# Attention and a gated feed-forward: x loaded turned and normalised so by GpSimd, projections dealt out anew, reciprocals of the row sums spread through DRAM

## What is computed

```python
x = x + tanh(g_xattn) * attention(layernorm(x), ctx, mask)     # 8 batches, 512 rows, D = 512, 16 heads of 32
x = x + tanh(g_ffn) * ffn(layernorm(x))
# attention: Q = layernorm(x) Wq' + bq, K = ctx Wk' + bk, V = ctx Wv' + bv, softmax with a mask, P V, output projection
# ffn:       r = sigmoid(mix_r Wr'), k = relu(mix_k Wk')^2, out = r * (k Wv'); mix = mu*x + (1-mu)*(x of the row before)
```

## Time and profile before

| | |
|---|---|
| median of three executions | 1231.34 us (1231.12 to 1231.93) |
| profiled execution | 1232.68 us, its span 1230.8 us |
| TensorE, VectorE, ScalarE, GpSimd busy | 1167.7, 942.5, 745.2, 237.4 us (95, 77, 61, 19%) |
| TensorE's granted clock, mean | 0.99 of full |
| DMA | 110.33 MB, 31% of the 16 engines' time |

### The profile page before, as it was taken

The page is one execution under the profiler, slowest core; times in us unless marked ns, Lnnn a source line. Parts: engine busy times, 40 slices in busy tenths (PEclk is TensorE's granted clock), DMA queues, the critical chain, the costliest instruction groups (busy, mean ns, idle before and its releaser), DMA issues.

```text
span 1230.8 us, 22178 instructions
## 1 busy us (share of the span) xinstructions
PE 1167.7 (95%) x7424; PEld 921.5 (75%) x7424; DVE 942.5 (77%) x2011; ACT 745.2 (61%) x1619; POOL 237.4 (19%) x427
## 2 busy tenths in 40 slices
PE   3999999999999999999999999977999999999997
PEld 2777776777777777777677777754888888888886
DVE  5778788788878887878878887879677677777763
ACT  4578778678768877877867876764432333233232
POOL 2030030030021003003003000024423433332431
PEclk9999999999999999999999999987999999999999
DMA  6433342253243333344225322452111311311200
GB/s 218 120 94 83 101 122 66 63 157 81 71 129 89 81 102 100 82 104 118 67 60 159 78 74 65 123 168 76 59 52 60 95 52 52 104 52 52 97 25 35
DMA packets 72703, 110.33 MB, mean 90 GB/s; under 512 B 14864, under 2 KB 23696, under 8 KB 72592
## 3 DMA queue, kind: packets, MB, share of 16 engines
q1 hardware_dynamic: 72592, 108.92, 31.1%
HBM read 41.76 MB, written 16.78 MB: 48 GB/s over the span
## 4 chain that ended last, share of the span: by engine, by line
PE 76%; DVE 9%; issue 6%; ACT 4%; DMA 4%; SPq 1%; POOL 0%; POOLq 0%; ACTq 0%; DVEq 0%
PE bank L445 24%; PE bank L509 14%; PE bank L476 12%; PE bank L521 10%; PE bank L502 7%; PE bank L485 6%; DMA x_rows<-x 3%; DVE neg_s L857 3%; ACT probs L681 2%; PE bank L491 2%; PE bank L575 1%; DVE pT L863 1%; DVE xh L973 1%; DMA pT<-wkT 1%; DVE ctx_sb L848 1%
## 5 line engine op out<-in xcount | busy, mean ns | idle before, releaser
L681 ACT ACTIVATE probs<-neg_s,negmax 128x512 f32<-128x512 f32 x512 | 367.9, 720 | 40.5 <-DVE negmax L857 39.4
L857 DVE CUSTOM_DVE_ANT_0 neg_s<-bank,mask_big 128x512 f32<-128x512 f32 x512 | 344.7, 683 | 19.2 <-PE bank L502 16.9
L509 PE MATMUL bank<-ident,probs 128*128 128x128 f32 x2048 | 314.8, 276 | 17.3 <-ACT probs L681 16.8
L509 PEld LDWEIGHTS bank<-ident,probs 128*128 128x128 f32 x2048 | 240.4, 141 | 75.6 <-ACT probs L681 40.7
L863 DVE COPY pT<-bank 128x512 f32<-128x512 f32 x256 | 176.5, 690 | 120.8 <-PE bank L509 119.7
L502 PE MATMUL bank<-k_stack,q_stack 96*128 96x512 f32 x512 | 243.3, 475 | 6.0 <-DVE negmax L857 5.9
L688 ACT COPY pT<-bank 128x512 f32<-128x512 f32 x256 | 149.4, 584 | 98.3 <-PE bank L509 92.5
L1068 POOL TENSOR_SCALAR var_eps<-mv 128x2 f32<-128x2 f32 (+1 forms) x24 | 18.5, 770 | 639.9 <-DVE mv L822 578.3
L521 PE MATMUL bank<-pT,v_sb 128*32 128x512 f32 x1024 | 118.5, 603 | 0.8 <-issue 0.5
L779 ACT ACTIVATE relu<-bank 128x512 f32<-128x512 f32 x32 | 19.2, 598 | 149.0 <-PE bank L445 149.0
L502 PEld LDWEIGHTS bank<-k_stack,q_stack 96*128 96x128 f32 x512 | 97.3, 190 | 11.2 <-DVE negmax L857 8.5
(11 more groups left out here) (110 smaller groups left out, 2125.1 us busy)
## 6 DMA issues: line engine op xcount, KB each, us to landing
k_stack<-k_hi SPq DMA_DIRECT2D x256, 64.0 KB, 2.0
q_stack<-q_hi SPq DMA_DIRECT2D x256, 64.0 KB, 2.0
x_rows<-x SPq DMA_DIRECT2D x8, 1024.0 KB, 6.6
cT_raw<-ctxT SPq DMA_DIRECT2D x8, 1024.0 KB, 5.8
k_stack<-k_lo SPq DMA_DIRECT2D x128, 64.0 KB, 2.0
q_stack<-q_lo SPq DMA_DIRECT2D x128, 64.0 KB, 2.0
ctx_dram<-ctx_sb SPq DMA_DIRECT2D x32, 256.0 KB, 2.1
c_raw<-ctx_dram SPq DMA_DIRECT2D x16, 512.0 KB, 5.1
```

The source lines that it names most:

```text
L509: mm = nc.tensor.transpose(pt_bank[i % 2][:, a * P:(a + 1) * P], probs[:, i % P_RING, a * P:(a + 1) * P], ident[:])
L681: nc.scalar.activation(probs[:, i % P_RING, :], neg_s[:, i % SM_RING, :], ACT.Exp, bias=negmax[:, k:k + 1], scale=-1.0, accum_out=den[:, g ...
L857: nc.vector.tensor_tensor_reduce(neg_s[:, i % SM_RING, :], s_bank[i % S_BANKS][:], mask_big[:, q, :], 1.0, 3e38, ALU.add, ALU.min, negmax[ ...
```

## The change

x is also passed turned (`xT_d`). From the second batch on, SyncE loads rows of x only for the statistics, one row of four to a partition, two tiles at a time, then x turned, also two at a time into the other half of the same buffer; mean and inverse root go to DRAM and come back spread over all partitions. GpSimd subtracts, scales and takes the rests of x and of the context; ScalarE rounds both at steps given by `x_hi_at` and `c_hi_at`. The T and C items are left in the prologue alone. K, Q and V are dealt out as one of each per group; Q 3 moves to steps 6 to 9 of group 1, so that x may be overwritten. The statistics of batch nb are taken at steps 8 and 10 of group 3 of batch nb-2 and steps 3 and 5 of group 0 of batch nb-1. The reciprocals are turned as they are (16 columns, one transpose), copied by VectorE at step 2 (into `ctx_sb`), stored to DRAM and loaded with 32 partitions for each head, four loads, which stand in SyncE's queue behind the first copies of Q; the product follows at step 7, and the context's store behind all of the stacking. At the end of the first stage the last product waits for its own trip. Semaphore counts, the order of the three side banks, and loops that were written as b in range(B-1) and a last one follow suit.

```diff
@@ -55,14 +55,11 @@
 
 
 PE_SIDE = [
-    parts("K", 1, 0, 1, 3, 4) | parts("V", 2, 6, 7, 8, 9, 10, 11) | parts("Q", 2, 12, 13, 14, 16),
-    parts("K", 2, 0, 1, 3, 4) | parts("V", 3, 6, 7, 8, 9, 10, 11) | parts("Q", 3, 12, 13, 14, 16),
-    {step: [("T", n, 0, 1)] for n, step in enumerate((0, 1, 3, 4))} | parts("K", 3, 5, 6, 7)
-    | parts("Q", 4, 9, 10, 12, 13, 14, 16),
-    parts("K", 4, 0, 1, 2) | parts("V", 0, 3, 4, 5, 6) | parts("V", 1, 7, 8, 9, 10)
-    | parts("Q", 5, 11, 12, 13, 14, 15, 16),
+    parts("K", 1, 0, 1, 3, 4) | parts("V", 1, 5, 6, 7, 8, 9, 10) | parts("Q", 2, 12, 13, 14, 16),
+    parts("K", 2, 0, 1, 3, 4) | parts("Q", 3, 6, 7, 8, 9) | parts("V", 2, 10, 11, 12, 13, 14, 15),
+    parts("K", 3, 0, 1, 3, 4) | parts("V", 3, 5, 6, 7, 8, 9, 10) | parts("Q", 4, 12, 13, 14, 16),
+    parts("K", 4, 0, 1, 3, 4) | parts("V", 0, 6, 7, 8, 9, 10, 11) | parts("Q", 5, 12, 13, 14, 16),
 ]
-PE_SIDE[2][TILES] += [("C", n, 0, 1) for n in range(CH)]
...
-STATS_STEPS = (8, 10, 12, 14)
-HI_STEP, LO_STEP = 1, 2
+def stats_at(nb):
+    return ((0, 0, 8), (0, 0, 10), (0, 1, 1), (0, 1, 3)) if nb == 1 else (
+        (nb - 2, 3, 8), (nb - 2, 3, 10), (nb - 1, 0, 3), (nb - 1, 0, 5))
+def x_hi_at(nb):
+    return ((0, 2, 0), (0, 2, 1), (0, 2, 7), (0, 2, 8)) if nb == 1 else (
+        (nb - 1, 1, 10), (nb - 1, 1, 11), (nb - 1, 2, 2), (nb - 1, 2, 3))
+def c_hi_at(nb):
+    return tuple((nb - 1, 2, i) for i in (11, 12, 13, 14))
+HI_STEP, LO_STEP, DIVIDE_STEP = 1, 2, 7
 HI_SIDE, LO_SIDE = out_side(0, HI_STEP), out_side(1, LO_STEP)
-EARLY = LO_STEP + 1
 C_ITEMS, T_ITEMS = [("C", n) for n in range(CH)], [("T", n) for n in range(TT)]
-PROLOGUE = C_ITEMS + [("K", 0)] + T_ITEMS + [("Q", 0), ("V", 0), ("V", 1), ("Q", 1)]
-NEXT_BATCH = C_ITEMS + T_ITEMS + [("Q", 4), ("K", 4), ("V", 0), ("V", 1), ("Q", 5)]
+PROLOGUE = C_ITEMS + [("K", 0)] + T_ITEMS + [("Q", 0), ("V", 0), ("Q", 1)]
+NEXT_BATCH = [("Q", 4), ("K", 4), ("V", 0), ("Q", 5)]
...
+        rden_rows = [ctx_sb[0:TILES, s, 0:P] for s in range(2)]
...
+            def load_rows(b, t):
+                if b == 1:
+                    sp.wait_ge(side_done, done(side_no(None, ("T", TT - 1))))
+                else:
+                    sp.wait_ge(x_lo, (b - 1) * CH)
+                if t >= 2:
+                    sp.wait_ge(bn_done, b * TT + t - 1)
+                sp.dma_start(x_rows[:, t % 2, :],
+                             x[bass.ds(b * S, S), :].rearrange("(p t) c -> t p c", t=TT)[t]).then_inc(rows_ld[t % 2], 16)
+            def load_xT(b, a):
+                if b > 1 or a >= 2:
+                    sp.wait_ge(x_lo, (b - 1) * CH + (a - 1 if a >= 2 else 0))
+                sp.dma_start(x_rows[:, 2 + a % 2, :], xT_d[bass.ds(b * D + a * P, P), :]).then_inc(xT_ld[a % 2], 16)
+            def broadcast_mean_rstd(b):
+                sp.wait_ge(mr_copy, b)
+                sp.wait_ge(pool_chain, (b + 1) * CHAIN)
+                sp.dma_start(mr_dram[b].rearrange("(k p t) -> p k t", k=2, p=P), mean_rstd[:]).then_inc(mr_st, 16)
+                sp.wait_ge(mr_st, b * 16)
+                sp.dma_start(x_rows[:, 0:2, :].rearrange("p k t -> p (k t)"),
+                             mr_dram[b:b + 1, :].to_broadcast([P, 2 * S])).then_inc(mr_ld, 16)
...
                 first = GH if n == GROUPS - 1 else GH - 1
                 stack_q(b, n, range(first))
+                if b * GROUPS + n > 1:
+                    load_rden(b * GROUPS + n - 2)
                 stack_k(b, n, (0,))
...
+            def store_rden(b, c):
+                sp.wait_ge(side_done, done(side_no(b, ("R", c))))
+                sp.dma_start(rden_dram[b * GROUPS + c].rearrange("(r q) -> r q", r=TILES),
+                             rden_rows[c % 2]).then_inc(rden_st, 16)
+            def load_rden(g):
+                sp.wait_ge(rden_st, (g + 1) * 16)
+                sp.wait_ge(ctx_done, g)
+                for j in range(GH):
+                    sp.dma_start(rden_bc[j * HD:(j + 1) * HD, :],
+                                 rden_dram[g:g + 1, j * S:(j + 1) * S].to_broadcast([HD, S])).then_inc(rden_ld, 16)
             def store_context(b, c):
-                sp.wait_ge(side_done, done(side_no(b, ("R", c))))
+                sp.wait_ge(ctx_done, b * GROUPS + c + 1)
                 sp.dma_start(ctx_dram[bass.ds(b * D + c * P, P), :], ctx_sb[:, c % 2, :]).then_inc(ctx_st[c % 2], 16)
             def batch(b):
                 for c in range(GROUPS):
-                    if c == 0 and not is_last(b):
-                        sp.wait_ge(side_done, done(b * SIDE_PER_BATCH + len(PROLOGUE) - 1))
-                        load_x(b + 1)
-                    if c:
-                        store_context(b, c - 1)
+                    if b + c == 0:
+                        load_rows(1, 0)
+                        load_rows(1, 1)
+                        load_xT(1, 0)
+                        load_xT(1, 1)
+                    if b + c:
+                        store_rden(*((b, c - 1) if c else (b - 1, GROUPS - 1)))
                     if not (is_last(b) and c == GROUPS - 1):
                         sp.wait_ge(s_mm, tile_no(b, c, 0) + HEAD)
...
                             sp.wait_ge(side_mm, mm_no(b, ("Q", c + 1)) + 1)
                             load_w2(0)
                         stack_group(b, c + 1)
+                    else:
+                        load_rden(b * GROUPS + c - 1)
+                    if b + c:
+                        store_context(*((b, c - 1) if c else (b - 1, GROUPS - 1)))
                     if c == 0 and not is_last(b):
                         load_ctx(b + 1)
+                    if b == 0 and c == 0:
+                        load_rows(1, 2)
+                        load_rows(1, 3)
+                    if c == (1 if b == 0 else 0) and not is_last(b):
+                        broadcast_mean_rstd(b + 1)
+                    if c == 1 and not is_last(b):
+                        load_xT(b + 1, 2)
+                        load_xT(b + 1, 3)
+                    if c == GROUPS - 1 and b + 2 < B:
+                        for t in range(TT):
+                            load_rows(b + 2, t)
+                        load_xT(b + 2, 0)
+                        load_xT(b + 2, 1)
...
+                if part == 0 and (kind, n) == ("Q", 4):
+                    pe.wait_ge(x_lo, (b + 1) * CH)
+                if part == 0 and (kind, n) == ("K", 4):
+                    pe.wait_ge(ct_lo, (b + 1) * CH)
...
-                    for q in range(TT):
-                        mm = nc.tensor.transpose(bank[:, q * P:(q + 1) * P],
-                                                 rden_rep[:, q].rearrange("p j d -> p (j d)"), ident[:])
+                    mm = nc.tensor.transpose(bank[0:TILES, 0:P], rden[:], ident[:])
...
-                pe.wait_ge(side_done, previous_r(b, c))
+                pe.wait_ge(ctx_done, b * GROUPS + c)
...
+            def x_rounded(nb, a):
+                act.wait_ge(side_mm, mm_no(nb - 1, ("Q", GROUPS - 1)) + 1)
+                act.wait_ge(x_hat, (nb - 1) * CH + a + 1)
+                nc.scalar.copy(act_hi[0][:, a, :], x_rows[:, 2 + a % 2, :]).then_inc(x_hi, 1)
+
+            def c_rounded(nb, a):
+                act.wait_ge(side_mm, mm_no(nb - 1, ("V", 3)) + 1)
+                act.wait_ge(c_ld, nb * 16 + 16)
+                nc.scalar.copy(act_hi[1][:, a, :], cT_raw[:, a, :]).then_inc(ct_hi, 1)
...
-                if t == 0:
-                    dve.wait_ge(x_ld, b * 16 + 16)
-                    dve.wait_ge(mv_done, b * TT)
-                nc.vector.bn_stats(stats[:, t, :], x_rows[:, t, :]).then_inc(bn_done, 1)
+                if b:
+                    dve.wait_ge(rows_ld[t % 2], ((b - 1) * 2 + t // 2 + 1) * 16)
+                else:
+                    dve.wait_ge(x_ld, 16)
+                dve.wait_ge(mv_done, b * TT)
+                nc.vector.bn_stats(stats[:, t, :], x_rows[:, t % 2 if b else t, :]).then_inc(bn_done, 1)
...
+                if kind == "R":
+                    dve.wait_ge(side_mm, mm_no(b, item) + 1)
+                    dve.wait_ge(ctx_st[n % 2], (b * 2 + n // 2) * 16 + DMA_HEAD)
+                    nc.vector.tensor_copy(rden_rows[n % 2], bank[0:TILES, 0:P]).then_inc(side_done, 1)
...
+            def divide(b, c):
+                g = b * GROUPS + c
+                dve.wait_ge(rden_ld, (g + 1) * GH * 16)
+                dve.wait_ge(pv_mm, g + 1)
+                nc.vector.tensor_tensor(ctx_sb[:, c % 2, :], pv_bank[:], rden_bc[:], ALU.mult).then_inc(ctx_done, 1)
...
-                dve.wait_ge(rden_ready, g + HEAD)
-                nc.vector.reciprocal(rden[:], den[:, c % 2, :]).then_inc(rden_calc, 1)
-                dve.wait_ge(rden_calc, g + 1)
-                src = rden[:].rearrange("p (j q) -> p q j", j=GH)[:, :, :, None].to_broadcast([P, TT, GH, HD])
-                nc.vector.tensor_copy(rden_rep[:], src).then_inc(rden_ready, 1)
+                nc.vector.reciprocal(rden[:], den[:, c % 2, :]).then_inc(rden_ready, 1)
...
```

(54 more changed lines are left out.)

149 lines of the change are left out of this document (62 added, 87 removed).

## The result

The changed kernel takes **1447.09 us** (median of four runs, 1446.53 to 1457.27) against 1231.63 for the kernel before beside it (1231.12 to 1232.03). The ratio is 1.177, with a 95% interval of 1.172 to 1.182. The forecast said 1367 with a range up to 1407. The direction was right; the size, +215 us where +136 was forecast, lies outside the range.

What follows compares the result with a forecast made beforehand. TensorE was taken to bound attention, thinly. Gain -51, product 17.5 + 38 + 2.8, Q3 40, statistics 67, clock 15, once-only 5 + 2: +136 us on the median of 1231.34, so 1367, range 1292 to 1407.

Steps and rivals of the forecast that it cites:

- the clock: TensorE at 1.2 GHz after the idle in group 3: 2.5 us for each of six, 15; bounds 0 and 6.8.
- S+6.1: SyncE's queue in group (3,1): the nine q copies end 6.1 us after S, the release of the reciprocals' store.
- S+10.2: SyncE's queue in group (3,1): the spread reciprocals are there 10.2 us after S, the release of their store.
- -51: The change's gain together: 48 us over seven batches, prologue -2.8, last batch's third group +0.3.
- the ends: Prologue loses a V item (-2.8); last reciprocals' trip delays VectorE (+4), early c_raw gives back about 2 (+2).
- (2): Attention: T gone and V items dealt anew, 4 x 23.25 = 93.0 against 99.9 a batch, 48 us over seven.
- up to 1.6 a batch if its cover is gone: ScalarE's roundings, four of 0.6, only move beside tiles 11 to 14: 0, up to 1.6 a batch uncovered.
- TensorE has about a tile in hand: Product at step 7: work in hand also covers the product (0.68), so wait minus 0.3 charged; group 0 2.5.
- the landing of the rows: Statistics at step 8 of group 3: row loads take 2.1 to land; VectorE stands 11.7 us, 67 charged for six batches.
- B: Only Q3's and the statistics' waits decide; the product's is hidden, the clock stays: 1294 us, chance 0.17.
- C: Neighbours' reserve absorbs the waits; late work is caught up before the PV block: 1211 us, chance 0.06.
- D: Low clock through the tiles after each stall (+26), x late in groups 1 and 2 (+14): 1407 us, chance 0.15.

Runs made afterwards that it cites:

- E7: The kernel before, with only the reciprocals' DRAM trip (one transpose per group) and the product at step 12: 1220.42 us, ratio 0.991.
- E3: E2 with all four heads' q copies ahead of k's for Q2 too: 1252.38 us, ratio 1.016.
- E5: E3 with the trip of mean and inverse root ahead of the 1 MB context load in batches 1 to 6: 1238.44 us, ratio 1.005.
- E9: E8 with the first batch's trip of mean and inverse root behind K's first head in SyncE's group 1: 1229.3 us, ratio 0.999.
- E8: E5 with V2 at steps 5 to 8 and Q3 at 9 to 12 of group 1, x's roundings moved too: 1235.76 us, ratio 1.003.
- E6: E5 with the reciprocals as in the kernel before (four transposes, product at step 2), leaving x's new way and dealing: 1230.87 us, ratio 0.998.
- E4: The changed kernel with idle identity transposes on TensorE at step 10, and more at step 11 of fourth groups, to keep its clock up: 1429.48 us, ratio 1.160.
- E2: E1 with the product with the spread reciprocals at step 12 instead of 7: 1282.28 us, ratio 1.041.
- E1: The changed kernel with the loads of batch b+2's first two row tiles ahead of the stacking copies in SyncE's group 3: 1392.13 us, ratio 1.130.
- E10: E7 with the product put back from step 12 to step 7: 1361.03 us, ratio 1.103.

## Why the prediction was right in direction and short in size

**What held.** All of the waits were where the prediction put them. The product waited 4.0 us on average in group 0, 3.2 in group 3 and 4.6 in group 2, where 3.1, 3 and 5 were said; the statistics stood 10.6 us behind a first wait of 2.7 in (3,3), where 8 to 9 behind 3 were said; ScalarE stood for the queries in all eight groups 1; the fourth group took 39.8 us where "34 us or more" was said, TensorE's share fell to 84% where some 85% was said, and the clock's digits fell below 9. One sign came in number but not in size: ScalarE's waits were to be 2 to 5 us, and seven of the eight were 0.5 to 1.2. The places on SyncE's queue, S+6.1 for the q copies and S+10.2 for the reciprocals, were right within half a microsecond. That part came from one sum: copies of 0.62 us, counted in the order in which the code issues them. The direction and nearly nine tenths of the waits' size (165 of 188.7 us) came from it. The gain of one transpose for four, 0.3 us a group, was right too (E7, 0.33).

**The thirty groups, as they came out.** 745.7 us became 952.4. No run has the change's own dealing without any wait, so its base is put together here: groups 0, 2 and 3 as in E3 (24.0, 24.8 and 23.8 us), group 1 at the 24.6 us of E5 without its wait (23.9 in batch 7, from E3), and (0,2) from E9. These come to about 728 us, an estimate, and a gain of 18. (E9, the one kernel measured with nearly no wait, has 743.4, but its group 1 is longer by E8's dealing.) The waits are 188.7 us (115.5 for the reciprocals, 64.3 for rows, 8.9 for queries). About 36 are left: the clock, and up to 4 us of the late x in (0,2). The sum: -18 + 189 + 36 = 207. The forecast had -51 + 3 (the prologue's share taken out), 165 and 20. So of the 69 us by which it was short there, 30 are a gain that did not come, 23 are waits, and 16 are mostly the clock; 9 more lie at the ends.

**The step that failed most: (2), "all four groups have the content of the second: 4 x 23.25 = 93.0".** Without waits the four groups of a batch sum to 97.2 us by the base above, against 99.9 before: a gain of 2.7 a batch, where 6.9 was said. (As measured, E6 has 98.5 and E9 98.6.) Only (6,3), which has neither statistics nor roundings, reaches 23.28; the row stands under E9. The others have the instructions of TensorE that the step counted, but not the neighbours' work in an even flow. Groups 0 and 3, in which the statistics of x stand, are 0.7 and 0.6 us longer; where they fall away ((7,0) and (6,3) of E3) the groups take 23.6 and 23.2. Group 1 is at 24.6 with x's roundings and 23.9 in batch 7 without. Group 2, with two roundings of x and four of the context on ScalarE, is at 24.8 to 24.9, with TensorE busy 23.8. The prediction had read the earlier trace rows that way, where the group without such work was the fastest and the one with the transposes of x lost 1.2 us in idling; it charged that idling to the transposes, which go, and not to the roundings, which stay. It had set aside "up to 1.6 a batch if its cover is gone" for ScalarE; 4.2 a batch are missing, statistics included.

**The second: the price of the waits.** "TensorE has about a tile in hand", with the wait charged less 0.3, is a small part of it. In (6,3), with no low clock, 2.58 us of waiting made 25.86 of 23.28: there is nothing in hand there. In E4's groups 1, also without low clock, about 0.3 us of the waits did not come through by the base above, as much as the prediction had taken off. The larger part is that in group 0 the forecast took 2.5 us, since VectorE would come later, and the wait measured 3.98. That is 10 us over seven batches.

**The third: the landing of the rows, taken as 2.1 us from the stores and context transfers of the earlier trace rows.** Row loads of the same size land in 3.9 us. With it the two waits of a fourth group are 13.3 us (2.7 and 10.6 in the timeline of (3,3)) where 11.2 was charged, some 17 us over all of those groups. Group 1 gave 4 back: its waits were 4.5 us where 4.2 to 5.2 was taken, and their parts had changed places, 3.3 for the product and 1.1 left for Q3, which stood in its shadow (E2).

**The fourth: the clock, of the right kind and sized too small.** 15 us were forecast, with 6.8 a batch as the bound. E4 gives 17 to 31, and the sum above leaves about 32. The reason given was that a long idle of TensorE brings a low stretch, but it did not come with the long waits alone. The groups 0 to 2, with waits of 3 to 6 us, had 4.9 us of it each on average, 112 of the 212 us.

**The ends** came to +1.8 before the thirty groups and +6.0 after them, where -2.8 and +2 were said. The first is within what varies: E1 to E5 have the changed kernel's prologue, and their thirty groups begin after 63.9 to 67.9 us, those of the kernel before after 64.7. But in none of them is the prologue 2.8 us shorter. The second is the product at step 7 of the last group and at the end of the stage, 10.8 us in two waits. With the product at step 12 (E2) these are 1.8 us, and the part behind the thirty groups takes 419.4 us, against 426.4 in the changed kernel and 420.4 in the kernel before.

Of the rivals, B ("only the two long waits decide") fell with E10: the product's wait alone costs more than 100 us. C fell: hardly any of the waits was absorbed. D ("the stalls breed more") had the time nearest to the result, 1407, and was right that the clock costs more than 15 us, but not by as much as its 41, and what it and the forecast have in common, step (2), is where most was lost.

What stays open: the 1.5 us by which group 2 stays above the floor, and the 0.7 that x adds in group 1, are put to ScalarE's roundings by the idle times of TensorE and by (7,1) alone. No kernel was run with these roundings taken away or spread over more steps. E9 is level with the kernel before, and E7 beats it by 0.9%; a kernel that has E7's reciprocals and a better schedule for x's roundings was not tried, nor was E9 with V2 and Q3 dealt out in another way.

## What to carry to other kernels

When a change puts a transfer on a queue that works in order, write down what stands in front of it there and add up the issue times: the landing of the reciprocals came out within half a microsecond that way, and moving the consumer five steps or the loads a few places made 141 and 55 us of difference without touching the transfers. Do not credit a group with the fastest group's time because TensorE has the same instructions in both; ask first why the others were slower, and whether what made them so goes away. When several waits fall in one stretch, the sum of the listed waits is not a list of what can be gained, since taking one away may bring another out of its shadow (1.2 us became 3.9 in (7,1)), and a queue that is no shorter than before falls behind shorter groups (8.3 us in (3,1), where both waits together had been 4.5).

## What the runs showed of the hardware beyond what was expected

- A small store behind a large load on the same queue is slow to be seen. The mean and deviation (4 KB), right behind the 1 MB load of the context, landed 5.1 to 6.6 us after issue in batches 1 to 6, and the queue stood 6 us for them. In batch 0, where the load is not just before them, it was 2.3 us, and in E5, with the load behind them, 1.8 to 3.1.
- Loads of 256 KB of x landed in 3.9 us, and stores of the context of the same size in 2.3 (medians, the DMA issues of the changed kernel). The loads were issued two or more behind one another, the stores alone, so that the two are not a clean comparison.
- TensorE's clock fell to 1.2 GHz in groups with waits of 3 to 5 us each: the windows have 0.88 and 0.89 in (3,1) and (3,2), while (6,3), with a single wait of 2.6 us, kept 1.00. Yet 178 us less of it (E4) were worth only 17 to 31 us, and in E10 123 us of it cost some 23.
- The issue of a load that repeats one row of DRAM over 32 partitions took 0.48 us (1.93 for four), and of a copy of 32 rows within SBUF 0.61.
